# A state-space mixer with other states for TensorE and GpSimd, a new order of its steps, and reordered transitions to the layers behind it

## The reference, cut to what matters

```python
# layer 0: x = x + mamba(ln_c(x)); then an FFN on the tokens; layer 1: x = x + displace(ln_c(x)); then an FFN
xin, z = split(xseq @ in_proj_w.T)                 # x: 8 images, 384 channels, 1024 positions; d_inner 768
u  = silu(causal_conv3(xin) + conv_b)
dt, Bm, Cm = split(u @ x_proj_w.T)                 # 24 + 16 + 16
dt = softplus(dt @ dt_proj_w.T + dt_proj_b)
h_t = exp(dt_t * A) * h_(t-1) + (dt_t * u_t) * B_t # 16 states for each of 768 channels, along 1024 positions
y_t = sum over the 16 states of h_t * C_t, + u * D
out = (y * silu(z)) @ out_proj_w.T
# FFN: layer norm, sign(W1 - mean of its group), absmax clipping to 8 bits, gelu, sign(W2 - mean), absmax clipping
```

## Time and profile before

| | |
|---|---|
| median of the runs shown | 3740.67 us (3735.48 to 3741.78) |
| profiled execution, its own time | 3742.58 us |
| its span, first to last instruction | 3740.8 us |
| VectorE, TensorE busy | 3316.0 us (89%), 3263.4 us (87%) |
| ScalarE, GpSimd busy | 2724.1 us (73%), 2691.5 us (72%) |
| mean granted TensorE clock | 0.954 |

### The profile page before, as it was taken

The page is one execution under the profiler, slowest core; times in us unless marked ns, Lnnn a source line. Parts: engine busy times, 40 slices in busy tenths (PEclk is TensorE's granted clock), DMA queues, the critical chain, the costliest instruction groups (busy, mean ns, idle before and its releaser), DMA issues. The chain is left out here.

```text
span 3740.8 us, 53922 instructions
## 1 busy us (share of the span) xinstructions
PE 3263.4 (87%) x15426; PEld 2203.4 (59%) x15426; DVE 3316.0 (89%) x3482; ACT 2724.1 (73%) x5202; POOL 2691.5 (72%) x2141
## 2 busy tenths in 40 slices
PE   5888889898988889798989888898779998889998
PEld 2555555555555556555555555555557776656776
DVE  3999998998999899999989998999976887976886
ACT  5887786787779678877977786788755654775653
POOL 3999998999899999989998998999931111561100
PEclk7999999999999999999999999999999999989999
DMA  3020211202020211202020211202020113641112
GB/s 138 10 96 18 97 61 47 89 18 90 19 96 20 96 52 55 90 18 89 19 97 18 97 50 57 89 18 80 34 94 18 69 53 127 228 185 51 69 36 85
DMA packets 83668, 259.01 MB, mean 69 GB/s; under 512 B 15212, under 2 KB 24044, under 8 KB 73092
## 3 DMA queue, kind: packets, MB, share of 16 engines
q1 hardware_dynamic: 82564, 254.04, 18.9%
q10 hardware_dynamic: 768, 1.05, 0.1%
HBM read 213.12 MB, written 41.95 MB: 68 GB/s over the span
## 5 line engine op out<-in xcount | busy, mean ns | idle before, releaser
L952 POOL TENSOR_TENSOR slot<-dtu,b_rep 128x512 f32<-128x512 f32 x1152 | 1450.5, 1276 | 100.7 <-PE ysum L451 100.0
L749 ACT ACTIVATE state<-dt,aneg 128x512 f32<-128x512 f32 x1152 | 786.4, 688 | 297.8 <-DVE slot L1061 253.9
L451 PE MATMUL ysum<-ident,slot 128*128 128x128 f32 x6144 | 839.7, 281 | 98.4 <-DVE slot L1061 66.0
L962 POOL TENSOR_TENSOR slot<-slot,c_rep 128x512 f32<-128x512 f32 x672 | 853.9, 1276 | 76.9 <-ACT carry L758 64.2
L451 PEld LDWEIGHTS ysum<-ident,slot 128*128 128x128 f32 x6144 | 717.1, 145 | 321.5 <-issue 172.6
L1061 DVE TENSOR_TENSOR slot<-state,c_rep 128x512 f32<-128x512 f32 x864 | 578.2, 671 | 0.0
L1053 DVE TENSOR_TENSOR_SCAN slot<-state,carry,slot 128x512 f32<-128x512 f32 x288 | 359.9, 1266 | 27.9 <-POOL slot L952 18.6
L1053 DVE TENSOR_TENSOR_SCAN slot<-state,slot 128x512 f32<-128x512 f32 x288 | 343.1, 1208 | 45.5 <-ACT state L749 43.3
L1053 DVE TENSOR_TENSOR_SCAN state<-state,carry,slot 128x512 f32<-128x512 f32 x288 | 363.6, 1275 | 0.7 <-issue 0.6
L1053 DVE TENSOR_TENSOR_SCAN state<-state,slot 128x512 f32<-128x512 f32 x288 | 347.2, 1216 | 1.9 <-ACT state L749 1.5
L569 PE MATMUL state<-diag_b,dtu_t 128*128 128x128 f32 x1536 | 224.1, 292 | 128.2 <-DVE slot L1061 71.2
(11 more groups left out here) (265 smaller groups left out, 6172.1 us busy)
## 6 DMA issues: line engine op xcount, KB each, us to landing
c_rep<-rows_of_b_and_c SPq DMA_DIRECT2D x64, 1024.0 KB, 4.9
xres_l<-between_layers SPq DMA_DIRECT2D x18, 1536.0 KB, 9.9
b_rep<-rows_of_b_and_c SPq DMA_DIRECT2D x32, 768.0 KB, 4.1
xn_l<-between_layers SPq DMA_DIRECT2D x13, 1536.0 KB, 7.1
b_rep<-rows_of_b_and_c SPq DMA_DIRECT2D x16, 1024.0 KB, 4.7
between_layers<-y SPq DMA_DIRECT2D x10, 1536.0 KB, 6.3
xn<-in_x SPq DMA_DIRECT2D x16, 768.0 KB, 4.5
xres<-in_x SPq DMA_DIRECT2D x16, 768.0 KB, 4.5
```

What stands on the lines that cost most here:

```text
L451: last = mm(ysum[:, cols], slot[:, (NS * k + n) % SLOTS, cols], ident[:], start=first and j == 0, stop=final, is_transpose=True, skip_grou ...
L749: af(state[:, (NS * k + n) % BANKS], dt[:, k], ACT.Exp, scale=aneg[:, k, n:n + 1]).then_inc(exp_done, 1)
L952: tt(slot[:, q % SLOTS], dtu[:, k % 2], b_rep[:, b_row(n)], ALU.mult).then_inc(dbu_done, 1)
L962: tt(slot[:, q % SLOTS], slot[:, q % SLOTS], c_rep[:, n], ALU.mult).then_inc(pool_mult_done, 1)
```

## The change

The states that TensorE drives become 7, 11, 14 and 15, with 11 and 14 turned (13 was turned before). GpSimd takes the product by C of state 8 and VectorE that of state 7. The counts stay: four drives, two of them turned, and seven products. Nearly every constant of the order is new. In the last chunk and at the entry of the layers, the means, signs, sums and out_proj are reordered, the wait for the last store is moved into `layers`, and `xres` and `y2` change places so that this is allowed. At the moved images the transposes stand behind `blocks_rest`, and the channel sum of d = 1 goes into `rstd`.

```diff
-POOL_N, POOL_LAG = (0, 1, 2, 4, 7, 9, 10), 6
-PE_N, TURN_N, SCALE_AHEAD, SCALED = (7, 11, 13, 15), (11, 13), 6, 2
-SUM_AT = (5, 4, 5, 7, 8, 8, 10, 11, 12, 13, 14, 12, 12, 13, 15, 15)
-COPY_Y, TURN_Y_AT, GATED_Y_AT = 5, (29, 38, 56, 72, 80, 1), (33, 40, 59, 76, 83, 3)
+POOL_N, POOL_LAG = (0, 1, 2, 4, 8, 9, 10), 6
+PE_N, TURN_N, SCALE_AHEAD, SCALED = (7, 11, 14, 15), (11, 14), 6, 2
+SUM_AT = (6, 5, 5, 10, 8, 10, 10, 11, 13, 13, 15, 12, 14, 14, 15, 15)
+COPY_Y, TURN_Y_AT, GATED_Y_AT = 5, (29, 34, 52, 72, 81, 1), (33, 39, 60, 75, 84, 1)
...
-LAST_OUT_IN, EARLY_OUT_AT, LATE_OUT_AT = (BX, BY, BZ), (86, 82, 84), (87, 88, 89)
+LAST_OUT_IN, EARLY_OUT_AT, LATE_OUT_AT = (BX, BY, BZ), (87, 82, 84), (88, 89, 90)
-MEAN_AT, CENTER_AT, SQUARE_AT, VAR_AT, RSTD_AT, SCALE_AT = 16, 20, 26, 25, 31, 29
-GATE_AT, GATE_IN = (18, 20, 36, 45, 66, 70), (BX, BZ, BY, BX, BY, BZ)
-IN_AT, IN_IN = (28, 31, 32, 38, 43, 47), (BY, BZ, BX, BX, BY, BZ)
-CONV_IN_AT, CONV_AT = (36, 37, 39, 47, 50, 54), (34, 35, 38, 45, 49, 51)
-SILU_AT = (31, 41, 56, 79)
+MEAN_AT, CENTER_AT, SQUARE_AT, VAR_AT, RSTD_AT, SCALE_AT = 15, 21, 25, 23, 29, 29
+GATE_AT, GATE_IN = (19, 20, 35, 46, 64, 70), (BX, BZ, BY, BX, BY, BZ)
+IN_AT, IN_IN = (30, 31, 33, 37, 44, 48), (BY, BZ, BX, BX, BY, BZ)
+CONV_IN_AT, CONV_AT = (36, 37, 40, 46, 48, 54), (34, 35, 38, 44, 49, 51)
+SILU_AT = (31, 41, 55, 79)
...
-XP_AT, XP_COPY_AT = 54, 59
-DT_AT, DT_IN = (56, 58, 63, 67, 4, 15), (BX, BY, BZ, BX, BZ, BZ)
-DT_READ_AT = (62, 65, 72, 74, 12, 24)
-DT_ADD_AT = (70, 72, 76, 93, 21, 30)
-DT_U_AT = 4
-TURN_U_AT, COPY_U_AT = (87, 8, 28, 39, 58, 77), (95, 18, 33, 49, 67, 82)
-DIAG_AT = (94, 4, 6, 7)
+XP_AT, XP_COPY_AT = 54, 61
+DT_AT, DT_IN = (56, 60, 68, 70, 2, 18), (BX, BY, BZ, BX, BZ, BZ)
+DT_READ_AT = (63, 64, 73, 77, 9, 24)
+DT_ADD_AT = (72, 73, 75, 94, 34, 41)
+DT_U_AT = 2
+TURN_U_AT, COPY_U_AT = (80, 8, 30, 42, 66, 75), (95, 16, 34, 50, 69, 80)
+DIAG_AT = (94, 9, 8, 0)
...
 # mixer, TensorE
+                    if not after and q == STEPS - 1:
+                        lead_mean(0)
...
-            lead_mean(0)
             lead_mean(1)
             turn_y(NCHUNK - 1, 1, KT - 1)
             lead_var(0)
-            for m in range(CT):
-                out_proj(NCHUNK - 1, 1, m, (KT - 1,), LAST_OUT_IN)
             lead_var(1)
+            out_proj(NCHUNK - 1, 1, 0, (KT - 1,), LAST_OUT_IN)
+            out_proj(NCHUNK - 1, 1, 1, (KT - 1,), LAST_OUT_IN)
             lead_total()
+            out_proj(NCHUNK - 1, 1, 2, (KT - 1,), LAST_OUT_IN)
...
 # mixer, ScalarE
             lead_rstd(0)
+            lead_rstd(1)
             for m in range(CT):
                 residual(NCHUNK - 1, m, LAST_OUT_IN)
-            lead_rstd(1)
-            for q in range(GROUPS):
-                lead_sign(q)
+            lead_sign(0)
...
 # mixer, SyncE: the wait for the last store; it is now in layers, in front of the
 # load of that image by SyncE and of down_bias(0, 0) on ScalarE
-            sp.wait_ge(x_stored, 16 * NCHUNK)
...
 # layers, ScalarE
             take_high(0, 1)
+            sign1(0, 1)
             act.wait_ge(bias_in, 64)
             for m in range(MT):
+                if m == 1:
+                    sign1(0, 2)
+                if m == 2:
+                    sign1(0, 3)
+                    sign1(0, 4)
...
 # layers, VectorE: the transposes of scale_of_d are now turn_of_d
                 if meets:
                     blocks_rest()
+                    turn_of_d(0)
...
 # layers, GpSimd, sum_tiles_d
                 elif d == 1:
-                    pool.wait_ge(down_full, DOWNS)
+                    pool.wait_ge(rstd_d, HALVES)
```

More of the change, by code:

```diff
@@ L82, in diag_n, with diag_order @@
     return [n for n in PE_N if n not in TURN_N]
+def diag_order():
+    return sorted(range(len(diag_n())), key=lambda i: ((DIAG_AT[PE_N.index(diag_n()[i])] + NS) % STEPS, i))
 def by_turn(c, q):
@@ L125, in __init__ @@
         self.x_first = [sem(f"x_first{h}") for h in range(HALVES)]
-        self.w2_in, self.x_summed = sem("w2_in"), sem("x_summed")
+        self.w2_in, self.x_summed, self.x_stored = sem("w2_in"), sem("x_summed"), sem("x_stored")
         self.mean_full, self.centered, self.squared, self.var_full = (
@@ L148, in mixer @@
         acc = sb("acc", [P, 3, T])
+        xres = sb("xres", [P, CT, T])
         u.append(sb("u1", [P, KT, T]))
@@ L164, in mixer @@
         halo_bias = sb("halo_bias", [P, KT, 2])
-        xres = sb("xres", [P, CT, T])
         sq = xres
@@ L197, in mixer @@
         x_loaded = [sem("x_loaded0"), sem("x_loaded1")]
-        xres_loaded, x_stored = sem("xres_loaded"), sem("x_stored")
+        xres_loaded, x_stored = sem("xres_loaded"), lead.x_stored
         mean_full, centered, squared, var_full = sem("mean_full"), sem("centered"), sem("squared"), sem("var_full")
@@ L554, in drive @@
                     if q < NS:
-                        pe.wait_ge(diag_b_set, len(diag_n()) * c + diag_n().index(n) + 1)
+                        pe.wait_ge(diag_b_set, len(diag_n()) * c + diag_order().index(diag_n().index(n)) + 1)
                 if (q < BANKS) == (h == 1):
@@ L898, in _ @@
             copy_b(0, 0)
-            for i in range(len(diag_n())):
+            for i in diag_order():
                 set_diag(0, 0, i)
@@ L1130, in _ @@
             gated_y(NCHUNK - 1, 1, KT - 1)
-            for q in range(GROUPS):
+            for q in range(3):
                 lead_sum(q)
             lead_scale(0)
+            lead_sum(3)
+            lead_sum(4)
+            lead_scale(1)
             lead_means()
-            lead_scale(1)
 GROUPS = 5
@@ L1175, in layers @@
         TILE = HW * 4
-        places = [("w1", CT * HID * 4), ("xn", CT * TILE), ("w2", MT * DM * 4), ("hid", MT * TILE), ("sq", CT * TILE),
-                  ("rstd", TILE), ("xres", CT * TILE), ("y2", CT * TILE), ("shared", 17 * TILE)]
+        places = [("w1", CT * HID * 4), ("xn", CT * TILE), ("w2", MT * DM * 4), ("y2", CT * TILE), ("hid", MT * TILE), ("sq", CT * TILE),
+                  ("rstd", TILE), ("xres", CT * TILE), ("shared", 17 * TILE)]
         arena = ctx.enter_context(nc.sbuf_tensor("arena", [P, sum(n for _, n in places) // 4], F32))
@@ L1207, in layers @@
         xsum = (put("xsum_0", [P, HW], "shared", 6 * TILE), put("xsum_1", [P, HW], "shared", 4 * TILE))
-        xsum_d = (xsum[0], put("xsum_d", [P, HW], "shared", 19 * TILE // 2))
+        xsum_d = [xsum[0], rstd] + [put("xsum_d", [P, HW], "shared", 19 * TILE // 2)] * (B - 1)
         gl = (put("gl_0", [P, AHEAD, HW], "shared", 7 * TILE, F32R), put("gl_1", [P, AHEAD, HW], "shared", 11 * TILE, F32R))
@@ L1318, in load_d @@
                     sp.wait_ge(stored, 16 * (MOVED[d] + 1))
+                if d < B and MOVED[d] == B - 1:
+                    sp.wait_ge(lead.x_stored, 16 * NCHUNK)
                 if d == B:
@@ L1496, in mean_of_d @@
                         pe.wait_ge(means_done, GROUPS + 3)
-                    mm(ph[h][:], mean_w[:], xsum_d[d > 0][:, half(h)], start=True, stop=True).then_inc(mean_d, 1)
+                    mm(ph[h][:], mean_w[:], xsum_d[d][:, half(h)], start=True, stop=True).then_inc(mean_d, 1)
             def var_of_d(d):
@@ L1625, in down_bias @@
                     act.wait_ge(down_full, MT * (f + 1))
-                    if f == FIRST[1]:
+                    if f == 0:
+                        act.wait_ge(lead.x_stored, 16 * NCHUNK)
+                    elif f == FIRST[1]:
                         act.wait_ge(stored_d, 16 * B)
@@ L2010, in scale_of_d, with turn_of_d @@
                                     ph[h][:].unsqueeze(1).broadcast_to([P, CT, T]), ALU.mult).then_inc(normed_d, 1)
+            def turn_of_d(d):
                 if d < B:
@@ L2063, in _ @@
                 scale_of_d(d + 1)
+                turn_of_d(d + 1)
                 if d == TOTAL_IN:
@@ L2134, in sum_tiles_d @@
                 elif d == 1:
-                    pool.wait_ge(down_full, DOWNS)
+                    pool.wait_ge(rstd_d, HALVES)
                 else:
                     pool.wait_ge(mean_d, HALVES * d)
-                o, a = xsum_d[d > 0], xd[d % 2]
+                o, a = xsum_d[d], xd[d % 2]
                 tt(o[:], a[:, 0], a[:, 1], ALU.add).then_inc(x_summed_d, 1)
```

4 lines of the change are left out of this document (2 added, 2 removed).

## The result

| | before | after |
|---|---|---|
| median of the runs | 3739.62 us | 3755.5 us |
| ratio, 95% interval | | 1.0037 [1.0027, 1.0048] |
| profiled execution: own time, span | 3742.58, 3740.8 us | 3749.33, 3747.5 us |
| first to last recurrence of the mixer | 2674.0 us | 2691.9 us |
| behind the last recurrence | 995.3 us | 985.8 us |

The change makes the kernel slower by 0.37%, some 14 us. One of the seven executions after took 3936.5 us at a clock of 0.823 and is left out of the ratio. I had forecast 3701 us and a range up to 3733. In the two traces the mixer is 17.9 us longer, and what lies behind it is 9.5 us shorter. So the mixer's part came out with the wrong sign.

The account below looks back on a forecast made before the run. VectorE was taken as the bound, so the mixer could win only its idle time, at most 13.4 us a pair of chunks. Terms of -4.4 a pair (-31), -1.3, -2.7 and -5.0 made -40: 3701 us, range 3673 to 3733.

Parts of the forecast that it names:

- Blocks k = 3 and 4 with h = 0: ScalarE is the slow engine and its items only move among each other; counted 0, bounds -2.3 and +1.5 us.
- Rival D: Longer waits for banks bring TensorE's half clock into the chunk heads too: +32 us, about 3733; chance 0.08.
- Head: Steps 0 to 15: new wait at `gated_y(5)`, recurrence 7 later, recurrence 11 earlier; -0.44 us a chunk, bounds -1.9 and +0.95.
- Mean, `turn_y(0)`: Mean's wait ends, -0.9 us with h = 0 and -0.3 with h = 1; `turn_y(0)`'s wait goes, -0.75 with h = 1.
- SiLU: ScalarE's SiLU block at step 55 makes recurrence 57 wait less with h = 0: -0.6 us, bounds -1.3 and 0.
- `dt_proj(2)` at 68: Moved from step 63, it no longer holds drive 71 up with h = 1: -1.0 us.
- Last chunk: Drive 91 stands ahead of the early out_proj, so the 2.65 us wait at recurrence 91 goes: -2.7 us.
- Mixer to layers: Layers begin 5.8 us sooner behind the mixer; four signs before tile 2 cost all but hidden 0.8: net -5.0 us.
- Moved images: The 1.56 us wait in the last down projection goes, but GpSimd's channel sum sets the chain: 0, bounds -1.6 and 0.
- The sum: Whole kernel: -31 - 1.3 - 2.7 - 5.0 = -40 us, giving 3701 us.

Follow-up runs that it names:

- e16: Changed kernel plus four unread matmuls before drive 71 and one before `dt_proj(0)`, in h = 0 chunks; 3715.99 us, 0.9943 to the kernel before.
- e7: Changed kernel with `gated_y(5)` back at step 3 and `dt_proj(4)` back at step 4; 3753.42 us, 1.0048 to the kernel before.
- e10: Kernel before with new transitions and only the priced moves (mean, centring, `in_proj(0)`, SiLU block, drive 91 ahead of early out_proj); 3724.2 us, 0.9959.
- e5: Changed kernel with `dt_proj(2)` at step 66 instead of 68; 3733.08 us, 0.9994 to the kernel before.
- e1: Kernel before, old states and constants, with the changed kernel's two transitions and last-steps order; 3734.55 us, 0.9981 to the kernel before.
- e6: Kernel before with five of the change's moves around drive 71 (`turn_u(4)`, its copy, `gate_proj(4)`, `dt_proj(2)`, `dt_proj(3)`); 3761.0 us, 1.0070.
- e12: Changed kernel with the copy of x_proj's result at step 59 instead of 61; 3762.29 us, 1.0073 to the kernel before.
- e13: Changed kernel plus eight unread matmuls before drive 71 in h = 0 chunks; 3748.29 us, 1.0020 to the kernel before.

## Why the prediction was wrong, by its own steps

**The step that failed** is "Blocks k = 3 and 4 with h = 0 ... I count 0", bounds -2.3 and +1.5. Measured at recurrences 62 to 75 with h = 0: +3.8 at 75, on average +2.2 at 62 to 65, and -0.6 at 71 to 74, so some +5 us a chunk. I looked at ScalarE's list alone, the engine that I called the slow one. The loss is TensorE's: `dt_proj(2)` and `gate_proj(4)` were its cover while drive 71 waits for the read-out of the carry. I applied "name the work that hides it" to what was moved away from a wait of VectorE, but not to what was moved out of an idle engine's gap.

**Rival D** (TensorE's clock, 0.08) had the mechanism, but in the heads and at 3733. It came in blocks 3 and 4, and cost 35 us by e16 against the changed kernel. Its sign came too: a clock below 0.95 in chunks with h = 0 (0.94 in the chunk from 1074.90). I had written that the waits here are of 2 us and less. That was a misreading: the trace before has 2.4 us ahead of drive 55 in every chunk of the loop with h = 0 and 2.9 with h = 1, and its clock stands at 0.50 for 226 of the mixer's 2674 us, mostly away from the loop's start. The change made that 297, the two fills 233; and the 3.9 us came from the change itself. The Trainium skill ("TensorE: Matmul & The Clock Gate", HAM oscillation — how this bites in real kernels) describes a wait between bursts of matmuls that makes the next burst start cold, each time anew. The trace of the changed kernel agrees at drive 71 (3.86 us idle, then 0.61 and 0.57), and its clock fell behind 1.69 us as well, in some chunks.

**Head.** Right in kind and, with h = 0, in size. `u<-pz` waits 1.3 (forecast 1.3); 7 waits 0.9 and 11 waits 0.3, together 2.5 instead of 3.2: -0.7 (forecast -0.44). With h = 1 the wait is 2.9 to 5.2 where the loop's body begins again, and I estimated 3. TensorE starts 2.7 us later than VectorE and at half clock; TensorE's row of that moment and VectorE's two of the kernel after:

```profile
909.46 4.49 PE L439 MATMUL px<-u,w_out 128*128 128x512 f32 x6 [5.26 <-issue]
...
906.77 3.63 DVE L1057 TENSOR_TENSOR_SCAN slot<-state,carry,slot 128x512 f32<-128x512 f32 x3 [3.29 <-ACT state L754]
915.28 0.69 DVE L1071 TENSOR_TENSOR u<-pz,gate 128x512 f32<-128x512 f32 x1 [4.88 <-PE pz L513]
```

Loop start and head together are 8.8 us instead of 9.0 (forecast -0.44). e7 shows that `gated_y(5)` at step 1 and `dt_proj(4)` at step 2 together cost nothing that can be measured (1.0048 without them, 1.0037 with); it doesn't tell them apart.

**Mean, `turn_y(0)`.** -0.7 with h = 0 (0.2 came at 22) and -0.95 with h = 1: in the changed kernel as forecast. In e10 the mean's term moved on to recurrence 23, so it wasn't worth what I gave it alone.

**SiLU.** -0.4 with h = 0 in the changed kernel (0.9 instead of 1.3; forecast -0.6), but +0.4 in e10: it hangs on the rest of the order.

**`dt_proj(2)` at 68, -1.0 with h = 1.** Measured -0.2: the 1.4 at 59 or 71 became 1.1 at 59, in every chunk. In e10 it went with `dt_proj(2)` left at 63. And in h = 0 this move is part of the loss: back at 66, it gave 16 us (e5). I had priced it in one half only.

**Last chunk.** Recurrence 91 no longer waits (-2.7), but 1.5 us at 70 are new; the chunk idles 1.9 less.

**Mixer to layers: -5.0.** Right. From the end of the last recurrence to the end, four traces with the old transitions average 993.4 us, the ten with the new and no fill 988.3: -5.1. In the profiled pair, the layers begin 16.5 us behind VectorE's last product instead of 21.95, -5.45 (forecast -5.8):

```profile
2761.61 1.27 DVE L1065 TENSOR_TENSOR slot<-state,c_rep 128x512 f32<-128x512 f32 x2
...
2779.38 2.86 ACT L1607 ACTIVATE xh<-xn_l 128x1536 fp32r<-128x1536 f32 x2 [0.29 <-PEq L139]
```

**Moved images: 0.** Right: the wait of 1.56 in the last down projection is gone, and the next one is as much longer, 8.69 instead of the 7.10 of the earlier trace rows.

```profile
3180.69 3.75 PE L1505 MATMUL ph_l<-rstd_l,mean_w_l 128*128 128x512 f32 x4 [8.69 <-POOL rstd_l L2161]
```

**The sum.** With both gaps filled, e16 is 0.9943, 21 us below the kernel before, against my 40. The transitions are 7 of it (my -5.0 held, and e1 doesn't have the move of drive 91), the mixer's order 14 where I had 35. A pair of chunks idles 2.8 us less than before (with h = 0 6.7 instead of 8.3, with h = 1 9.3 instead of 10.5) where I had 4.4; new waits of 0.9 to 2 us at 76 and 78 are most of the difference. So with the clock kept up in blocks 3 and 4 the sign holds, and the mixer's size was more than twice too large.

**Still open.** Why the clock falls behind 1.7 us in one chunk and not in the next with identical work (in e6 behind 3.15 us and not behind 3.14), and why in e12 it falls at 52 to 55 and stays low longer behind drive 71. Of the mixer's 17.9 us, 12.9 are waits; the other 5 are spread over VectorE's some 2700 instructions, a few ns each, and over gaps too short to list; I didn't pursue them.

## What to carry to other kernels

When work is moved along an engine's list, ask not only which wait it leaves but which idle gap it filled: the work behind the gap may then run at half TensorE's clock. Compare the duration of one kind of matmul on both sides of a gap; when it doubles, count the rest of that burst at the low clock before you judge its order. If no useful work fits, a few matmuls that nobody reads, no longer than the gap, can pay: 35 us of 3755 here, while a fill twice as long gave most of it back.

## What the runs showed of the hardware

- Behind 3.86 us idle the clock stood at 0.50 from 1199.6 to 1209.7, although TensorE was busy in all 10.10 us of it (windows above). There it fell only when TensorE was already at work again: from 1198.3 to 1199.5 it was still 1.00.
- Behind the same 1.69 us idle it was 1.00 in one chunk and 0.51 in another of the same execution. Filled to 0.83 us, it stayed at 1.00 there in all seven of the loop. In e6 it was 0.56 behind 3.15 us and 1.00 behind 3.14.
- e5's executions spread with it: from 3727 us at a mean clock of 0.953 to 3750 at 0.943. Not every spread does: e13's ran from 3740 to 3756 us at 0.953 to 0.956. And e16's five runs stayed within 3714.5 to 3723.3 and those of the kernel before beside it within 3732.2 to 3742.4.
